# Closing norm of batch 0 in the run-out of a state-space loop, and rope units ordered anew, in a two-layer transformer kernel

## The reference, cut to what matters

```
x = x + layernorm(L0_attn(layernorm(x)))
x = x + layernorm(L0_ffn(layernorm(x)))
x = x + layernorm(L1_attn(layernorm(x)))      # the state-space layer
x = x + layernorm(L1_ffn(layernorm(x)))       # the head MLP, channels permuted
```

```
x1, x2 = x[..., ::2], x[..., 1::2]
out = stack([x1 * cos - x2 * sin, x1 * sin + x2 * cos], axis=-1)
```

## Time and profile before

| | |
|---|---|
| median of 3 runs | 2691.8 us (2689.99 to 2694.04) |
| profiled execution, its own time | 2689.63 us |
| its span | 2687.8 us |
| TensorE busy | 2484.4 us, 92% |
| DVE, ACT, POOL busy | 1765.7 (66%), 1420.0 (53%), 1512.5 (56%) |
| granted TensorE clock, mean | 0.97 |

### The profile page before, as it was taken

How to read it: one execution, slowest core, us unless ns; L and a number is a source line. 1 busy time by engine, 2 the same in 40 slices (tenths; PEclk the granted TensorE clock), 3 DMA queues, 4 the chain that set the end, 5 groups by cost and what they waited for, 6 DMA issues and landing times. The chain is left out here.

```text
span 2687.8 us, 37367 instructions
## 1 busy us (share of the span) xinstructions
PE 2484.4 (92%) x12664; PEld 1813.3 (67%) x12664; DVE 1765.7 (66%) x3153; ACT 1420.0 (53%) x2796; POOL 1512.5 (56%) x1306
## 2 busy tenths in 40 slices
PE   7989995799799779999999999999999999999948
PEld 3464443444587667878878878878778878887734
DVE  2144454577423687777777777777777777777764
ACT  2200002656222286676676676676676676776603
POOL 0043365454101248678678678678678678678641
PEclk9999997899899899999999999999999999999978
DMA  4012320000210163353353342352352342352210
GB/s 162 0 38 75 117 63 32 1 1 1 86 51 21 64 194 105 89 158 100 94 158 97 97 157 95 100 154 93 102 156 91 100 158 91 99 161 91 69 47 32
DMA packets 143483, 241.86 MB, mean 90 GB/s; under 512 B 28352, under 2 KB 48576, under 8 KB 143168
## 3 DMA queue, kind: packets, MB, share of 16 engines
q1 hardware_dynamic: 143296, 239.48, 28.3%
HBM read 232.08 MB, written 7.34 MB: 89 GB/s over the span
## 5 line engine op out<-in xcount | busy, mean ns | idle before, releaser
L1755 ACT ACTIVATE mix<-mix,sc 128x128 f32<-128x128 f32 x1024 | 310.8, 389 | 3.0 <-DMA sc<-head_scal 3.0
L1925 DVE SCALAR_TENSOR_TENSOR feat<-ps,chan,feat 128x511 f32<-128x511 f32 (+2 forms) x384 | 283.7, 739 | 1.8
L2057 POOL TENSOR_TENSOR xend<-xdt,sc 128x384 f32<-128x384 f32 x128 | 107.0, 836 | 315.8 <-DVE xdt L1888 315.8
L98 PE MATMUL ps<-xt_hi,w_in_hi 128*128 128x512 f32 x640 | 266.9, 417 | 11.7 <-ACT sg L1745 3.5
L1914 DVE TENSOR_TENSOR mix<-mix,cb 128x512 f32<-128x512 f32 x256 | 270.6, 1062 | 1.2 <-ACT mix L1761 1.2
L99 PE MATMUL ps<-xt_lo,w_in_hi 128*128 128x512 f32 x640 | 253.2, 396 | 0.0
L100 PE MATMUL ps<-xt_hi,w_in_lo 128*128 128x512 f32 x640 | 253.1, 395 | 0.0
L2073 POOL TENSOR_TENSOR w_in_lo<-w_in_raw,w_in_hi 128x512 fp32r<-128x512 f32 x158 | 211.6, 1340 | 62.2 <-ACT w_in_hi L1710 62.2
L1959 DVE TENSOR_TENSOR y_lo<-y,y_hi 128x512 fp32r<-128x512 f32 x128 | 184.4, 1441 | 80.4 <-ACT y_hi L1771 80.1
L98 PE MATMUL ps<-xt_hi,w_g_hi 128*128 128x512 f32 x512 | 212.7, 415 | 4.6 <-DVE feat L1925 4.6
L1602 PE MATMUL ps<-w_o_hi,y_hi 128*128 128x512 f32 x512 | 206.9, 404 | 7.0 <-DVE x L1974 3.6
(11 more groups left out here) (278 smaller groups left out, 5946.3 us busy)
## 6 DMA issues: line engine op xcount, KB each, us to landing
mix<-row_cum SPq DMA_DIRECT2D x128, 512.0 KB, 5.7
w_in_raw<-in_w_conv_in SPq DMA_DIRECT2D x160, 256.0 KB, 3.0
w_g_raw<-in_w_gate_in SPq DMA_DIRECT2D x128, 256.0 KB, 3.4
ecb<-row_ecum SPq DMA_DIRECT2D x256, 96.0 KB, 3.4
w_o_raw<-in_w_out SPq DMA_DIRECT2D x64, 256.0 KB, 3.0
w<-in_w_c2q SPq DMA_DIRECT2D x16, 768.0 KB, 4.4
w<-in_w_c2q SPq DMA_DIRECT2D x16, 512.0 KB, 3.6
wqkv<-in_w_qkv SPq DMA_DIRECT2D x1, 3072.0 KB, 13.9
```

Of the source, the lines that this page charges most:

```text
L98: pe.matmul(out, a_hi, b_hi, start=(n == 0), stop=False)
L1755: last = act.activation(m, m, ACT.Relu, bias=sc[:, b, CUM, z, 2 * i + e:2 * i + e + 1], scale=-1.0)
L1925: dve.scalar_tensor_tensor(out=to, in0=ps[:, j % 2, 0:S - back], scalar=chan[:, bb % B, j, K1 - 1 - back:K1 - back], in1=to, op0=ALU.mult, ...
```

## The change

- Key rope: the ring `raw` gets 4 places instead of 2 (`RAWK`), and DVE issues `first` two units ahead: units 0 and 1 before the first step, unit u + 2 in step u.
- Query rope: of a unit's four rotations POOL keeps two; DVE does the other two in `turn`, ahead of the sums. Keys keep four on POOL.
- Closing norm: the block is gone. Batch 0's part is issued in the run-out's steps: statistics in k = 1, aggregation in k = 2, POOL's power in k = 3, scaling in place in k = 4, sum with the old x in k = 5; then the head's own statistics of batch 0 in k = 6, aggregation in k = 7 and power in k = 8. The old x is loaded in k = 0 in two DMAs into the buffers of the projection's weights.
- Head: starts with the normalised tiles of batch 0; `take` is built behind them; batch 1's closing norm (`last_measured`, `last_added`; POOL adds tiles 6 and 7) and the head's statistics of it (`half_measured`) stand between `xp` copies. Tiles 4 to 7 are turned in steps 2 and 3. All z go through bank 1, so a down product waits for the cut of the z before it. The head shares `xt_hi` and `xt_lo` with the layers before.

```diff
@@ attention
-    NI = 4 * QT
+    NI, RAWK = 4 * QT, 4
...
+            def rots_before(u):
+                return 4 * min(u, NK) + 2 * max(u - NK, 0)
+
+            def rotate(eng, u, i, side, table):
+                kind, n, t, e = units[u]
+                heads = KV0 if kind == "k" else HF
+                pair = unit[:, u % 2, 0:heads, :].rearrange("p h (j e) -> p h j e", e=2)
+                which, z = (0, t % ZB) if kind == "k" else (1, t % 2 * 2 + e)
+                return eng.tensor_tensor(rot[:, i, 0:heads, :], pair[:, :, :, side],
+                                         table[:, which, z:z + 1, :].to_broadcast([P, heads, HD // 2]), ALU.mult)
...
-                        dve.wait_ge(rot_done, 4 * (u + 1))
                         dve.wait_ge(unit_done, u + 1)
+                        if kind == "q":
+                            for i, side, table in ((2, 0, sin), (3, 1, cos)):
+                                rotate(dve, u, i, side, table).then_inc(late_rot, 1)
+                            dve.wait_ge(late_rot, 2 * (u + 1 - NK))
+                        dve.wait_ge(rot_done, rots_before(u + 1))
...
+                        first(0)
+                        first(1)
                         for u in range(NK + 1):
+                            if u + 2 < NK:
+                                first(u + 2)
                             if u < NK:
-                                first(u)
                                 measure(u)
@@ state_space, SP
+                if not main and k == 0:
+                    wait(sp, "proj_ready", g, 0, 0)
+                    for bn in range(B):
+                        sp.dma_start(st.x_old[bn], st.x_saved[:, bn * ZB:(bn + 1) * ZB, :]).then_inc(st.x_back, 16)
@@ state_space, DVE, at the end of a step
+                if not main and k == 1:
+                    for t in range(ZB):
+                        dve.bn_stats(core.stats[:, t, :], acc[:, t, :]).then_inc(st.fin.stats, 1)
...
+                if not main and k == 4:
+                    dve.wait_ge(st.fin.rstd, 1)
+                    for t in range(ZB):
+                        dve.tensor_scalar(acc[:, t, :], acc[:, t, :], core.mv[:, t, 0:1], core.rstd[:, t:t + 1],
+                                          ALU.subtract, ALU.mult).then_inc(st.fin.scaled, 1)
+                if not main and k == 5:
+                    dve.wait_ge(st.x_back, 16 * B)
+                    for t in range(ZB):
+                        dve.wait_ge(st.fin.scaled, t + 1)
+                        dve.tensor_tensor(x[:, t, :], acc[:, t, :], st.x_old[0][:, t, :], ALU.add).then_inc(st.fin.added, 1)
+                if not main and k == 6:
+                    for t in range(ZB):
+                        dve.wait_ge(st.fin.added, t + 1)
+                        dve.bn_stats(core.stats[:, t, :], x[:, t, :]).then_inc(st.fin.stats, 1)
...
@@ state_space, POOL, at the end of a step
+                if not main and k in (3, 8):
+                    pool.wait_ge(st.fin.vare, 1 + k // 8)
+                    pool.tensor_tensor(core.rstd[:, 0:ZB], core.vare[:, 0:ZB], core.half[:, 0:ZB], ALU.pow).then_inc(st.fin.rstd, 1)
@@ head_mlp, DVE
+                dve.wait_ge(st.fin.rstd, 2)
                 norm(0)
                 norm(1)
                 for t in range(HALF):
                     low(t)
-                    norm(t + 2)
-                for t in range(HALF):
-                    keep_xp(t)
-                    low(HALF + t)
-                    if HALF + t + 2 < NT:
-                        norm(HALF + t + 2)
+                    if t + 2 < HALF:
+                        norm(t + 2)
+                gather_matrix()
+                last_measured()
+                keep_xp(0)
+                last_added()
+                keep_xp(1)
+                half_measured()
+                norm(HALF)
+                norm(HALF + 1)
+                keep_xp(2)
+                low(HALF)
+                norm(HALF + 2)
+                cut_z(0)
+                low(HALF + 1)
+                norm(HALF + 3)
+                keep_xp(3)
+                low(HALF + 2)
+                cut_z(1)
+                low(HALF + 3)
@@ head_mlp, TensorE
+        LATE_TURNS = {2: (HALF, HALF + 1), 3: (HALF + 2, HALF + 3)}
...
-                    if j == 1:
-                        pe.wait_ge(xt_lo_done, NT)
-                    if j >= 2:
-                        pe.wait_ge(z_done, j - 1)
+                    if j >= 1:
+                        pe.wait_ge(z_done, j)
+                    else:
+                        pe.wait_ge(xt_lo_done, HALF)
```

More of the change, by code:

```diff
@@ L73, in sem, with stage_end @@
         return self.sems[-1]
-    def stage_end(self):
-        self.nc.clear_and_free_semaphores(self.sems)
+    def stage_end(self, alive=()):
+        self.nc.clear_and_free_semaphores([s for s in self.sems if s not in alive])
         self.nc.all_engine_barrier()
-        self.sems = []
+        self.sems = list(alive)
 class NormSems:
@@ L172, in __init__, with all @@
         self.added = core.sem(name + "_added")
+    def all(self):
+        return [self.stats, self.aggr, self.vare, self.rstd, self.scaled, self.added]
 def add_vector(dve, core, s, t, src, scaled):
@@ L681, in rope @@
                             pool.wait_ge(rope_done, 2 * u)
[L682 to L685, removed]
-                                               table[:, which, z:z + 1, :].to_broadcast([P, heads, HD // 2]),
-                                               ALU.mult).then_inc(rot_done, 1)
+                        turns = ((0, 0, cos), (1, 1, sin), (2, 0, sin), (3, 1, cos))
+                        for i, side, table in turns if kind == "k" else turns[0:2]:
+                            rotate(pool, u, i, side, table).then_inc(rot_done, 1)
                     def rope_k():
@@ new lines, in spread, with last_measured @@
+                def spread(sems, turn):
+                    for i, t in enumerate(late):
+                        dve.wait_ge(sems.stats, turn * HALF + i + 1)
+                        dve.bn_aggr(core.mv[:, t, :], core.stats[:, t, :]).then_inc(sems.aggr, 1)
+                    dve.wait_ge(sems.aggr, turn * HALF + HALF)
+                    dve.tensor_scalar(core.vare[:, HALF:], core.mv[:, HALF:, 1], LN_EPS, None, ALU.add).then_inc(sems.vare, 1)
+                def last_measured():
+                    for t in late:
+                        dve.bn_stats(core.stats[:, t, :], x[:, t, :]).then_inc(st.fin.stats, 1)
+                    spread(st.fin, 2)
@@ new lines, in last_added @@
+                def last_added():
+                    dve.wait_ge(st.fin.rstd, 3)
+                    for t in late:
+                        dve.tensor_scalar(x[:, t, :], x[:, t, :], core.mv[:, t, 0:1], core.rstd[:, t:t + 1],
+                                          ALU.subtract, ALU.mult).then_inc(st.fin.scaled, 1)
+                    for t in (HALF, HALF + 1):
+                        dve.wait_ge(st.fin.scaled, t + 1)
+                        dve.tensor_tensor(x[:, t, :], x[:, t, :], st.x_old[1][:, t - HALF, :], ALU.add).then_inc(st.fin.added, 1)
@@ L2298, in norm, with half_measured @@
+                def half_measured():
+                    for t in late:
+                        dve.wait_ge(*((st.fin.added, t + 1) if t < HALF + 2 else (late_added, t - HALF - 1)))
+                        dve.bn_stats(core.stats[:, t, :], x[:, t, :]).then_inc(ln.stats, 1)
+                    spread(ln, 0)
                 def norm(t):
-                    if t == 0:
+                    if t == HALF:
                         dve.wait_ge(ln.rstd, 1)
@@ L2409, in _ @@
                         high(step - 2)
+                    if step in LATE_TURNS:
+                        keep_turned(LATE_TURNS[step][1])
             @blk.tensor
```

129 lines of the change are left out of this document (57 added, 72 removed).

## The result

The changed kernel takes 2670.07 us, the median of 4 runs (2667.62 to 2671.43). The kernel before took 2690.89 us in the same comparison (4 runs, 2689.22 to 2694.04). The ratio is 0.9921, with a 95% interval of 0.9908 to 0.9934: 21.3 us faster by the ratio, 17.8 to 24.8 by its ends. The forecast was 2668.7, within 2662 to 2680. The profiled execution of the changed kernel took 2671.36 us and has a span of 2669.6, so the two profiled spans differ by 18.2.

A forecast was written before the change was run, and what follows sets the result against it. TensorE, busy 92% of the span, was taken as the bound, so only its idle stretches could give much. Terms -3.3 - 7.7 - 13.1 + 1.0 = -23.1 gave 2668.7 us against the median, range 2662 to 2680.

The forecast's parts named there:

- the three signs of being wrong: A query period of 5.2, an accumulation over 10 us late, or a TensorE wait of 6 us in the head.
- A: Key rope: evicting key units two ahead lets TensorE start near 184.3, not 190.99; -3.3 us.
- the lower bound, -2.0: Key rope: TensorE keeps only 2.0 us if the new pause before the third item costs the clock again.
- Rival 3: Key rope: early eviction does nothing, as the third item awaits preparation and the clock takes the rest; 2672.0 us, chance 0.07.
- B: Query rope: sharing rotations between POOL and DVE shortens the periods from 5.23 to about 3.9 and 4.75; -7.7 us.
- the port on the last unit alone: Query rope's last unit: DVE's rotations beside POOL's are not free, so the four take some 2.2 us, not 1.4.
- Rival 1: Query rope: the port holds also against POOL's power, period 5.3, nothing gained from sharing rotations; 2676.4 us, chance 0.08.
- rival 4: Query rope: each DVE rotation is held for a whole POOL instruction, 2.1 instead of 0.38; slower, 2698.8 us, chance 0.03.
- C: State-space run-out: batch 0's closing norm inside it, accumulation 4.6 later, closing block gone; together -13.1 us.
- closing block: State-space end: the stretch from 2585.48 to 2604.89 shrinks to the barrier alone, 1.70; -17.7 us.
- Rival 2: Run-out: the inserted norm lies wholly on the path, accumulation 14.4 later instead of 4.6; 2678.5 us, chance 0.10.
- D: Head: batch 0's norm starts at once, batch 1's closing follows, fifth gather at 34.3 instead of 33.5; +1.0 us.

The follow-up runs named there:

- third_item: Changed kernel with the query convolution's third item also prepared ahead of or inside the key rope; 2664.76 us, ratio 0.9907 against the kernel before.
- keys_only: Kernel before plus only the key units evicted two ahead with four raw buffers; 2685.85 us, ratio 0.9988.
- queries_only: Kernel before plus only the query units' four rotations shared two and two between DVE and POOL; 2685.85 us, ratio 0.9985.
- rotations_dve: Changed kernel with all four rotations of a query unit on DVE, POOL keeping the power; 2668.95 us, ratio 0.9923 against the kernel before.
- early_stats: Changed kernel with batch 0's four statistics, aggregation and POOL's power moved to earlier steps of the run-out; 2668.61 us.

## Why the prediction was right

The time, 2670.07, is 1.4 from the forecast, and the rivals all fell. That it is so near is in part luck. All four terms were too hopeful: in the profiled pair they come to -1.8, -6.2, -10.0 and +1.9, that is -16.1 for -23.1. The stretches that the change doesn't touch gave 2.1 more (-18.2), and the medians differ by 20.8, nearer to the forecast than any sum of the terms. Of the signs named, a barrier of about 1.8 and TensorE's wait of 3.5 behind the third gather came; the query periods were 4.2 and 4.8 for 3.9 and 4.7, the fifth gather 35.4 after the block's start for 33 to 35, the accumulation later than said, and the stage behind the query rope came 7.3 us earlier, not 11. None of the three signs of being wrong came.

- **A, -3.3.** Measured -1.8 in this pair, and -2.4 as the mean of six profiles against three without it. The start of the items, the pause and its cause were as told, and the third item started 36.5 us behind the first key eviction, 36.6 by the forecast. The mis-sized term is the clock behind the pause: I took it only as the lower bound, -2.0. Without A the third item starts 40.6 to 40.9 us behind that eviction, so all six have 4.3 in hand there, and the third item then takes 6.9 to 10.0 us, 9.2 in this execution, at a granted clock of 0.50 at first; it took 6.9 in the kernel before. Rival 3 falls: with A the stretch is 236.5 to 239.8 in six profiles, without it 240.6 to 241.3 in three, and third_item shows more behind the same wait. keys_only's ratio alone would not do, since its profile gained more outside A's stretch than in it.
- **B, -7.7.** Measured -6.2. The mis-sized step is the period without evictions, forecast 3.9 and measured 4.20: the period follows POOL, whose two rotations took 1.65, not 1.4, since the second stands behind DVE's, and whose power took 1.74 to 1.81, not 1.64. (DVE's second rotation took 0.95, not 0.38, off that path.) The period with evictions was 4.81 for 4.75. The last unit gained 0.7, not 1.0 (from its power to `k_twice` 5.66, before 6.39). I had allowed for the port on the last unit alone, and it acts on every unit without evictions. Rival 1 falls, since DVE's instructions beside POOL's power kept their length, and with it rival 4, which wanted 2.1 us a rotation; a DVE rotation is held by one of POOL's, but for 0.6 us once a unit, and off the path. Inside the loop it was worth nothing, as said: queries_only's stretch to the query eviction is not shorter.
- **C, -13.1.** The gain of the closing block is -17.60, forecast -17.7. The accumulation came 6.1 later than in profiles with the same run-out (104.2), 7.6 later than in the profiled kernel before; forecast 4.6. By the steps: `xdt` +1.6 (forecast 1.74), power +1.0 (1.1), work behind the last y_lo +2.0 (1.8). The step that failed is the one that I did not have: the late `xdt` makes TensorE wait longer, and its next products run at the low clock, +1.5. The other 1.5 between the two counts is not the change's but the clock's too (102.7 in the profiled kernel before, 104.2 in both others). In an earlier step, 63 us behind the 16th mask, TensorE waits 2.0 us ahead of its `mix` products, in every profile. Behind that wait the granted clock stayed at 1.00 in the kernel before and in rotations_dve, and fell to 0.50 in the eleven other profiles. The kernel before, then keys_only; the first window of each holds the wait, the second the products behind it:

```profile
2542.00:2544.80 2.80, 1.35 (x18) 1.00 0.03 11
2544.80:2546.80 2.00, 2.00 (x13) 1.00 0.27 94
```

```profile
2534.00:2536.80 2.80, 1.42 (x18) 0.92 0.03 8
2536.80:2538.80 2.00, 2.00 (x9) 0.50 0.28 97
```

So C is about -11.5. The scalings behind the last y_lo took 2.86, not the 2.0 of my "POOL is idle after its last square": POOL's `y_sq_sum` ran on to 2574.26, and the first scaling stood for it. The other terms made up for that. Rival 2 falls, as early_stats shows.

- **D, +1.0.** Measured +1.9. First gather 9.2 after the start (forecast 9.3), first tile of batch 1 at 21.5 (21.9), TensorE waiting from 18.6 to 22.1 (18.6 to 22.4), all near. The fifth gather came at 35.4, not 34.3, since tile 7's low part stands behind a z on DVE. I counted that handshake on TensorE's bank and not on DVE's list. "From the fifth gather on nothing changes" holds but for the clock: 47.4 to 51.0 us over twelve profiles and the one before, all alike there.

## What to carry to other kernels

Size a part of a change by the stretch between two events that lie on its path, and add the stretches: single parts of 2 to 6 us in a kernel whose time wanders by 8 can't be sized by times. If work is moved ahead for an engine that waits, ask at once what that engine waits for next: more than half the gain of the early evictions lay behind the next item's preparation, and a few instructions put into idle places gave it back. Work moved beside a busy GpSimd is priced by what it takes beside it, instruction by instruction, since a mean hides the one that waits; with the clock, price a new wait twice, for itself and for the matmuls that follow it, and measure such a part in several executions.

## What the hardware showed that I had not expected

- Behind like waits TensorE's granted clock was 0.50 in some executions and 1.00 in others: behind a wait of 2.9 to 4.6 us before the third item, behind one of 3.6 us before the first (window means of 0.79 to 1.00), and behind one of 2.0 us in the run-out, where it was worth 1.5 us. Which, is not settled by these runs. The first made one stretch 236.5 or 239.8 us long.
- A stretch with the same instructions, `k_twice` to the 16th mask, took between 2021.2 and 2029.4 us. Part of it is the granted clock between 500 and 600 us; what sets it stays open.
- DVE and GpSimd took turns. A DVE rotation of 0.42 beside one of POOL's took 0.96 and ended 0.3 us behind it; a scaling of one tile (128 x 512) took 0.54 where it was not held and 1.2 to 1.5 where a POOL instruction was under way, again ending 0.3 us behind it. Means of 0.72 and 1.07 over four of them were mixtures of the two.
- Beside POOL's power DVE's rotations stayed at 0.42, and the power went from 1.64 to 1.93.
